# Expert lists from 64 lanes and 16 marks in four column tiles, and the second bias added on TensorE

## The reference

```python
def balanced_assignment(scores):          # scores: 8192 tokens x 8 experts
    T, E = scores.shape
    C = T // E                            # 1024
    taken = jnp.zeros((T,), dtype=bool)
    parts = []
    for e in range(E):
        s = jnp.where(taken, -jnp.inf, scores[:, e])
        _, idx = jax.lax.top_k(s, C)
        parts.append(idx)
        taken = taken.at[idx].set(True)
    return jnp.concatenate(parts)
...
    routed = feat[sort_by_expert].reshape(E, C, D)
    h = layer_norm(routed, ln_g, ln_b)
    h = jax.nn.gelu(jnp.einsum('ecd,edf->ecf', h, w1) + b1[:, None, :])
    h = jnp.einsum('ecf,efd->ecd', h, w2) + b2[:, None, :]
    out = routed + h
```

## Time and profile before

| | |
|---|---|
| median of 3 runs | 1599.43 us (1596.18 to 1599.5) |
| profiled execution | 1599.61 us |
| its span | 1597.8 us |
| first expert stage | 628.9 to about 934 us of the span |
| second expert stage | 1258.9 to about 1569 us |
| TensorE busy over the span | 1191.3 us (75%) |
| VectorE busy over the span | 972.9 us (61%) |
| mean granted TensorE clock | 0.838 of full speed |

### The profile page before, as it was taken

One profiled execution on the slowest core, in us unless ns is written; L12 is line 12 of the kernel. 1 busy time (PEld: TensorE's weight loads), 2 busy tenths in 40 slices (PEclk: granted clock), 3 DMA queues, 4 the chain that ended last, 5 costly groups with the idle time before them and its releaser, 6 DMA issues. The chain is left out here.

```text
span 1597.8 us, 34549 instructions
## 1 busy us (share of the span) xinstructions
PE 1191.3 (75%) x11004; PEld 800.7 (50%) x11004; DVE 972.9 (61%) x2744; ACT 696.4 (44%) x1450; POOL 773.6 (48%) x744
## 2 busy tenths in 40 slices
PE   1899999999999967477887904549996548878880
PEld 0344444444444446256666703449996426656660
DVE  4566666767666654888874043925555488878302
ACT  0666667676766624322222405545552612222240
POOL 0577777777777720045556720035550014446661
PEclk9999999999999965577887956869996557888795
DMA  5000000000000022012112140000003101111217
GB/s 141 1 1 0 0 0 0 0 0 0 0 0 0 1 60 77 3 27 60 50 43 55 53 118 11 0 10 0 0 0 86 50 14 39 45 42 50 56 52 217
DMA packets 67972, 54.50 MB, mean 34 GB/s; under 512 B 12865, under 2 KB 57281, under 8 KB 67905
## 3 DMA queue, kind: packets, MB, share of 16 engines
q1 hardware_dynamic: 51392, 32.70, 7.5%
q0 software_dynamic: 8192, 16.79, 3.7%
q10 hardware_dynamic: 8320, 4.19, 0.9%
HBM read 32.69 MB, written 20.97 MB: 34 GB/s over the span
## 5 line engine op out<-in xcount | busy, mean ns | idle before, releaser
L319 POOL TENSOR_TENSOR patt_aa<-patt_aa,causal_aa 128x512 f32<-128x512 f32 x256 | 319.1, 1273 | 100.8 <-DVE patt_aa L443 100.8
L443 DVE TENSOR_TENSOR patt_aa<-p_second_aa,first_aa 128x512 f32<-128x512 f32 x384 | 247.5, 686 | 163.1 <-ACT first_aa L376 161.3
L1231 POOL DMA_INDIRECT rows_e<-norm_rows,index_e x128 | 123.6, 966 | 369.5 <-DVE index_e L955 329.5
L376 ACT ACTIVATE first_aa<-p_first_aa 128x512 f32<-128x512 f32 x384 | 208.4, 596 | 146.8 <-PE p_first_aa L534 143.0
L534 PE MATMUL p_first_aa<-q_t_aa,k_t_aa 32*128 32x512 f32 x768 | 217.4, 642 | 30.4 <-ACT first_aa L376 30.4
L534 PE MATMUL p_second_aa<-q_t_aa,k_t_aa 32*128 32x512 f32 x768 | 233.3, 642 | 0.0
L1143 PE MATMUL p_cnt_e<-reach_e,ones_e 128*128 128x240 bf16 x448 | 89.8, 337 | 102.9 <-DVE reach_e L1001 102.8
L1246 POOL DMA_INDIRECT ffn_rows<-yb_e,index_e x128 | 130.6, 1020 | 58.1 <-issue 32.3
L1077 PE MATMUL p_h_e<-rows_t_e,w_e 128*128 128x512 f32 x256 | 148.6, 710 | 0.2
L553 PEld LDWEIGHTS p_z_aa<-patt_aa,v_aa 128*32 128x32 f32 x3072 | 74.9, 109 | 123.9 <-issue 68.2
L1194 ACT ACTIVATE hid_e<-p_h_e,b_e 128x512 f32<-128x512 f32 x128 | 87.9, 688 | 102.6 <-PE p_h_e L1077 102.4
(11 more groups left out here) (229 smaller groups left out, 2278.6 us busy)
## 6 DMA issues: line engine op xcount, KB each, us to landing
norm_rows<-norm_n SPq DMA_DIRECT2D x32, 256.0 KB, 2.3
w_e<-L_ffn_w SPq DMA_DIRECT2D x32, 256.0 KB, 2.8
buf_r<-ffn_rows SPq DMA_DIRECT2D x16, 512.0 KB, 5.7
out<-x ACTq DMA_DIRECT2D x8, 512.0 KB, 8.2
rows_e<-norm_rows,index_e POOLq DMA_INDIRECT x128
ffn_rows<-yb_e,index_e POOLq DMA_INDIRECT x128, 2.3
b_e<-L_ffn_b SPq DMA_DIRECT2D x16, 64.0 KB, 3.7
lanes<-c_lanes SPq DMA_DIRECT2D x1, 256.0 KB, 3.0
```

The costliest lines, as they stand in the source:

```text
L319: pool.tensor_tensor(patt[n % LAG][:, b, :, :], patt[n % LAG][:, b, :, :], causal[:, None, :].broadcast_to([P, 4, P]), ALU.mult).then_inc( ...
L376: act.activation(first[n % 2][:, b, :], p_first[b][:], ACT.Identity).then_inc(first_copied, 1)
L443: dve.tensor_tensor(patt[n % LAG][:, b, :, :].rearrange("p h q -> p (h q)"), p_second[(2 * n + b) % ROOMS][:], first[n % 2][:, b, :], ALU. ...
L1231: pool.indirect_dma_start(rows[lpar][:, j, :], None, norm_rows, bass.IndirectOffsetOnAxis(ap=list_of(l, lpar)[:, j:j + 1], axis=0)).then_i ...
```

## The change

There are four parts.

A place is split into 64 lanes and 16 tiles. `lane_of` has half its size, eight operations of 512 elements; `tile_is` keeps 1024 elements, and `tile_of` becomes two operations of 1024, one for each part of the token's number.

The list matmuls swap their operands: `tile_of` (32 columns) is the stationary one and `lane_of` (64 columns, at a step of 8 bf16 elements) the moving one. The product of tile t goes to rows 32(t mod 4) and up of `p_part`, so four column tiles of the array are used in turn. VectorE copies `p_part` to `quarters` (`copy_parts`), and two fp32 matmuls with a constant `fold` (`list_fold`) sum the four parts into `p_idx` in its old form.

The second bias is added on TensorE: each `down` begins with a matmul of `first_row` (ones in row 0, zeros elsewhere) with `b2`. ACT copies the result straight to `yb`, and GpSimd's addition, the buffer `y` and the semaphore `y_ready` are gone.

The pieces and windows are laid out anew, and `sixteenth`, `fold` and `first_row` are made by six more VectorE operations at the start of the stage.

```diff
-        p_idx = p_list[:, 2 * TILES:2 * TILES + 2 * SLOTS]
+        p_part = p_list[:, 2 * TILES:2 * TILES + LOW]
+        p_idx = p_list[:, 2 * TILES + LOW:2 * TILES + LOW + 2 * SLOTS]
...
+                dve.tensor_copy(sixteenth[:, 0:SLOTS, :], eighth[:, 0:SLOTS, :]).then_inc(sv, 1)
+                dve.tensor_scalar(sixteenth[:, SLOTS:HIGH, :], eighth[:, 0:SLOTS, :], float(SLOTS), None, ALU.add).then_inc(sv, 1)
+                for half in range(2):
+                    dve.tensor_reduce(fold[:, half, :, :], k["ident"][:].rearrange("p (c k h s) -> p h k s c", c=4, k=2, h=2)[:, half, :, :, :],
+                                      AX.X, ALU.add).then_inc(sv, 1)
+                dve.memset(first_row[:], 0.0).then_inc(sv, 1)
+                dve.wait_ge(sv, SETUP - 1)
+                dve.memset(first_row[0:1, :], 1.0).then_inc(sv, 1)
...
-                        dve.tensor_tensor(tile_of[:], tile_is[:], place[:], ALU.mult).then_inc(tiles_done, 1)
+                        for kind in range(2):
+                            dve.tensor_tensor(tile_of[:, kind, :, :], tile_is[:], place[:, kind * SLOTS, None, :].broadcast_to([P, HIGH, TILES]),
+                                              ALU.mult).then_inc(tiles_done, 1)
...
-                        dve.tensor_tensor(lane_of[:, c, :, :], low_b[:, None, c * per:(c + 1) * per].broadcast_to([P, P, per]),
-                                          lanes[:], ALU.is_equal).then_inc(lanes_done, 1)
+                        for n in (2 * c, 2 * c + 1):
+                            dve.tensor_tensor(lane_of[:, n, :, :], low_b[:, None, n * per:(n + 1) * per].broadcast_to([P, LOW, per]),
+                                              lanes[:, 0:LOW, :], ALU.is_equal).then_inc(lanes_done, 1)
+
+                    def copy_parts():
+
+                        dve.wait_ge(parts_done, l + 1)
+                        dve.tensor_copy(quarters[:], p_part).then_inc(parts_copied, 1)
...
-                        windows = [[slots], [parts, narrow], [tiles], chunks[0:2], chunks[2:4], chunks[4:6], chunks[6:8], [result]]
+                        chunks = [lambda c=c: lane_chunk(c) for c in range(CHUNKS // 2)]
+                        windows = [[slots], [parts, narrow], [tiles_are, chunks[0]], [tiles], [chunks[1]], chunks[2:4], [copy_parts], [result]]
...
+                        pe.matmul(p_y[t // 4][:, (t % 4) * D:(t % 4 + 1) * D], first_row[:], b2[par][:], start=True, stop=False)
                         for f in range(FC):
                             mm = pe.matmul(p_y[t // 4][:, (t % 4) * D:(t % 4 + 1) * D], hid[:, f, t * P:(t + 1) * P], w2[par][:, f, :],
-                                           start=(f == 0), stop=(f == FC - 1))
+                                           start=False, stop=(f == FC - 1))
...
-                            mm = pe.matmul(p_idx, lane_of[:, n, :, j], tile_of[:, :, t], start=(t == 0), stop=(t == TILES - 1))
...
+                        for j in range(2 * per):
+                            t = 2 * n * per + j
+                            c = j % 4
+                            mm = pe.matmul(p_part[32 * c:32 * c + 32, :], tile_of[:, :, :, t].rearrange("p k h -> p (k h)"),
+                                           lane_of[:, t // per, :, t % per], start=(t < 4), stop=(t >= TILES - 4))
...
+                    def list_fold(l):
+
+                        pe.wait_ge(parts_copied, l + 1)
+                        for half in range(2):
+                            mm = pe.matmul(p_idx[64 * half:64 * half + 64, :], quarters[:], fold[:, half, :, :].rearrange("p k s -> p (k s)"),
+                                           start=True, stop=True)
+                        mm.then_inc(listed, 1)
...
-                        pieces = [[], [], [], [lambda: turn_rows(0)], [lambda: turn_rows(1), lambda: up(0), lambda: up(1)],
-                                  [lambda: up(2), lambda: up(3)], [lambda: up(4), lambda: up(5)],
-                                  [lambda: up(6), lambda: up(7)], [lambda: down(0), lambda: down(1)],
-                                  [lambda: down(2), lambda: down(3)]]
+                        pieces = [[], [], [], [lambda: turn_rows(0)], [lambda: turn_rows(1), lambda: up(0)],
+                                  [lambda: up(1)], [lambda: up(2), lambda: up(3)], [lambda: up(4), lambda: up(5)],
+                                  [lambda: up(6), lambda: up(7), lambda: down(0)],
+                                  [lambda: down(1), lambda: down(2), lambda: down(3)]]
...
-                    pool.wait_ge(y_copied, 2 * c + h + 1)
-                    pool.tensor_tensor(yb[par][:, part, :], y[:, part, :], b2[par][:, None, :].broadcast_to([P, SLOTS // 2, D]),
-                                       ALU.add).then_inc(y_ready, 1)
-                    wait_apart(pool, y_ready, 2 * c + h + 1, wait_passed)
+                    wait_apart(pool, y_copied, 2 * c + h + 1, wait_passed)
```

81 lines of the change are left out of this document (41 added, 40 removed).

## The result

The changed kernel takes 1562.6 us (median of 4 runs, 1560.4 to 1564.3) against 1598.4 of the kernel before beside it: ratio 0.9777, 95% interval 0.976 to 0.9795. It is 35.8 us faster. The profiled execution has a span of 1562.6 us, against 1597.8, with the clock at 0.856 on average.

What follows compares the result with a forecast made beforehand. A TensorE-VectorE handshake, each pacing parts of a turn, with GpSimd's additions holding VectorE. A stage: 1.1 - 1.3 - 0.3 - 5.2 - 3.9 = -9.6 us; two stages -19 from 1599.4 give 1580.5 us, range 1565 to 1603.

Steps and rivals of the forecast that it cites:

- Step 1: In a full turn, dropping GpSimd's additions gives VectorE back 3.2 us, and GpSimd 2.1 us for each addition.
- C2 to C4: From the start of pass 2's count to pass 4's in a turn; forecast 6.1 us against 9.69, so -3.5.
- Step 2: VectorE's list work: lane operations halve to 512 elements, a pair falling from 1.29 us to about 0.75.
- Step 3: Bias on TensorE: one more fp32 matmul a tile, 0.23 us each; +0.45 us between counts 0 and 1, +0.15 between 1 and 2.
- Step 4: The tail, from a turn's last count to the next turn's first: two more `up` and biased tiles, +2.9 us.
- Setup: Ahead of a stage's first search: six more operations, +1.1 us.
- the end of the stage: After the full turns: index wait, clock, list, biased tiles and last additions together -3.9 us a stage.
- the full turn: A turn with search, list and compute: -1.3 us, four turns a stage giving -5.2 us.
- C4 to C7: From the start of pass 4's count to pass 7's: 11.1 us against 12.44, so -1.3, list matmuls at 50 ns.
- rival B: List matmuls cost 41 ns or less, and TensorE's shorter idle gaps keep the clock up: 1563 us; chance 0.21.
- C: Rival: the moving operand's 16-byte step slows each list matmul; at 107 ns the time is 1615 us; chance 0.15.
- D: Rival: the lengthened stretch behind a turn's last count eats the whole gain, 1594 to 1600 us; chance 0.14.

Runs made afterwards that it cites:

- 1644 group: Four runs where the kernel before took 1643.9 us: changed kernel with idle GpSimd addition (1.005), fill (1.0093) or idle matmuls (1.0051); kernel before with idle matmuls (1.0006).

## Why the prediction was off

**The mechanism was right.** GpSimd's addition held VectorE, and its time stood in GpSimd's chain: the bias alone gives 28 of the 36 us, and an addition that nobody reads takes the whole gain back. Step 1 forecast C2 to C4 at 6.1 us, measured 6.19 in that turn and -3.6 us on the mean of four. Step 2: lane pairs 0.76 (0.75 forecast). Step 3: C0 to C1 +0.45, as forecast. Step 4: the tail +2.6 on the mean, against +2.9. Setup +1.1, as forecast.

**How the miss divides.** The two profiles differ by 35.4 us, 16.2 more than the 19.2 forecast: 5.8 at the ends of the stages, 8.8 in the eight full turns, 1.6 before them. No wait and no path was wrong; terms of the sum were mis-sized, those of the half clock and of the list above all.

**The first step that failed is the end of the stage (-3.9 forecast, -8.1 and -5.5 measured).** In the first stage the index wait gave 4.1 us (3.6 forecast) and the last additions and tiles 0.6 (0.7), as they should. What failed are the three terms about the clock and the list in between: six `up` -2.4 instead of -1.2; list and fold -1.1 instead of +0.2; eight biased tiles +0.2 instead of +1.4. I carried over the half clock that the tiles show in the earlier trace rows, and never asked what made it fall there. For the tiles the runs show it: the old list ahead of them. The new list keeps the clock, and with it in four column tiles the tiles are at 9.04 in every stage traced outside the 1644 group. For the six `up` they don't. In the second stage these took 8.62 us, at 0.66 of the clock, 1.0 more than in the kernel before (7.61), behind a wait of 2.9; in the second profile of the same kernel they took 6.2 behind the same wait (TensorE's row of it in the first profile, which answers to the row at 849.19 above):

```profile
1463.16 8.69 PE L1101 MATMUL p_h_e<-rows_t_e,w_e 128*128 128x512 f32 x12
```

So the 2.4 us that the first stage won there were in part luck. Against the first stage that end gave 3.4 us less in the `up` and 1.0 more in the tiles, which took 9.83 before.

**The second is the full turn (-1.3 us forecast, -2.2 measured on the mean of the first stage's four turns), and in it C4 to C7 (-1.3 forecast, -1.8 measured, 12.24 to 10.46).** The rest of that miss is the tail (0.3) and C0 to C4 (0.2). The list matmul costs 30 ns from one start to the next and 36 to 43 with the time until what follows starts, not 50: rival B's first half came true, at 31 to 41 ns 48 of them are 0.4 to 0.9 us. The other half of B did not: the clock still falls in each turn, though in turn 3 the stretch at half is 6.9 us long instead of 10.2, with one `up` in it instead of two. I also took from turn 3 what I gave to four turns. Its change is -2.0; that of the others is -2.8, -1.4 and -2.6, where C2 to C4 had been 9.91 in turns 4 and 6. In the second stage the four turns gave 10.3 us, with the long turn 5 in both kernels.

**What I had put down to the wrong edit.** I counted the new pieces as a cost (two `up` more in the tail, +2.0, and out of C4 to C7) and the list as the gain. With the bias in place the pieces alone take C4 to C7 from 12.4 to 10.0, the mean of the first stage's four turns; with the new list it is 10.5. The four `up` behind C7 run at full clock, 0.93 us each; two of them stood before in the stretch at half, where two cost 3.62. That trade I had in both terms, but as one and a half `up` at half clock of four, and never priced against the old list.

**The rivals.** C's 107 ns exists, in one column tile (104 to 124 measured), and cost more than the 1615 us that it said (1645.3); four tiles hide it. The prediction has it that no row of before shows a moving operand with such a step. One does, with a longer step: the old list moves `tile_of[:, :, t]`, 16 columns 128 bytes apart. By the price in one column tile, 112 ns for 64 columns, they would be about 28 of the 60 ns of its pair (an estimate). That GpSimd's indirect transfers hold nothing is not quite so either: `cand`, 0.31 us otherwise, takes 0.36 to 0.51 us in 14 of the 18 cases in which it meets one in the changed kernel. D didn't occur. The range's lower end, 1565, came from adding only a part of B; it lacked the case that the list itself holds the clock up at the stage's end.

What stays open: where in the profile the 5 us lie by which the kernel with the old list and new pieces is faster, why in one stage of twelve the tiles behind the old list ran at full clock, what property of the matmuls the clock goes by, when the six `up` at a stage's end run at half, and what the engines lacked in the 1644 group.
